# Decoder layer with sorted expert tokens: normalised rows scattered as fp16 halves, sorted tiles turned by the loading DMA, routing tables on GpSimd, two banks for z

## The reference

```python
x = x + attn(layernorm(x), Wqk, bqk, Wv, bv, Wu, bu, Wo, bo, ln_g, ln_b)   # linear attention, 16 heads, gated by silu(u)
x = x + xattn(layernorm(x), tokens, ctx, ctx, ctx)
x = x + ffn(layernorm(x), W_up, W_gate, W_down)
# attn: q = k = elu(x Wqk + bqk); kv = k^T v per head; out = (u * layernorm(q kv; ln_g, ln_b)) Wo + bo
# xattn: expert e = min(token // 6250, 3); W = ctx[e];  y = (silu(n W^T) * (n W^T)) W^T, of the token's own expert
# ffn: ternary weights, q(w) = clip(round(w / mean|w|), -1, 1) * mean|w|; y = (silu(n up^T) * (n gate^T)) down^T
```

## Time and profile before

| | us |
|---|---|
| median of 3 runs (764.87 to 765.67) | 765.36 |
| the profiled execution | 763.66 |
| its span, first to last instruction | 761.9 |
| TensorE busy | 715.7 (94%) |
| VectorE busy | 386.8 (51%) |
| ScalarE busy | 273.1 (36%) |
| GpSimd busy | 131.0 (17%) |
| mean granted TensorE clock | 0.988 of full speed |

### The profile page before, as it was taken

One profiled execution on the slowest core, in us unless ns is written; L12 is line 12 of the kernel. 1 busy time (PEld: TensorE's weight loads), 2 busy tenths in 40 slices (PEclk: granted clock), 3 DMA queues, 4 the chain that ended last, 5 costly groups with the idle time before them and its releaser, 6 DMA issues.

```text
span 761.9 us, 11591 instructions
## 1 busy us (share of the span) xinstructions
PE 715.7 (94%) x3948; PEld 381.1 (50%) x3978; DVE 386.8 (51%) x655; ACT 273.1 (36%) x426; POOL 131.0 (17%) x171
## 2 busy tenths in 40 slices
PE   8998999899899869999998999999999999999993
PEld 6565457457446546666554444444444444444441
DVE  5669766846836746655465333343334333342232
ACT  4365545536436334454322332222222222222220
POOL 4202124404606840000010000020001100020002
PEclk9999999999999999999999999999999999999998
DMA  8924026006207369650102000020001100010001
GB/s 238 343 72 149 1 101 208 23 8 216 108 1 275 126 199 390 240 153 29 29 15 42 15 14 11 4 69 15 14 14 25 58 14 14 15 55 1 0 0 55
DMA packets 48182, 63.99 MB, mean 84 GB/s; under 512 B 25360, under 2 KB 25360, under 8 KB 47120
## 3 DMA queue, kind: packets, MB, share of 16 engines
q1 hardware_dynamic: 43792, 50.89, 21.0%
q0 software_dynamic: 4352, 12.60, 4.3%
HBM read 46.69 MB, written 12.59 MB: 78 GB/s over the span
## 4 chain that ended last, share of the span: by engine, by line
PE 82%; DVE 6%; POOL 4%; issue 3%; ACT 2%; SPq 1%; DMA 1%; DVEq 0%; ACTq 0%; POOLq 0%
PE bank L1342 29%; PE bank L1070 28%; PE bank L1352 14%; PE bank L1063 4%; PE bank L1263 3%; PE bank L1227 2%; DVE late L759 1%; POOL sorted_ids L330 1%; PE bank L1241 1%; POOL sorted_tokens L322 1%; DMA stage<-in_L_attn_Wv_dram 1%; DVE region L606 1%; POOL sorted_residual L326 1%; SPq L190 1%; DVE st L598 1%
## 5 line engine op out<-in xcount | busy, mean ns | idle before, releaser
L1342 PE MATMUL bank<-w_att,region 128*128 128x512 f16 (+1 forms) x1024 | 231.3, 379 | 1.0 <-issue 1.0
L1342 PEld LDWEIGHTS bank<-w_att,region 128*128 (+1 forms) x1024 | 100.1, 98 | 122.0 <-issue 1.5
L1036 DVE SCALAR_TENSOR_TENSOR tmp<-tmp,hk,bank 128x512 f32<-128x512 f32 x64 | 47.8, 747 | 161.6 <-PE bank L1342 161.1
L1352 PE MATMUL bank<-region,tmpA 128*128 (+1 forms) x474 | 116.9, 379 | 1.6
L309 POOL TENSOR_SCALAR ve<-mv 128x1 f32<-128x1 f32 (+1 forms) x37 | 9.5, 256 | 485.0 <-DVE mv L974 336.2
L1070 PE MATMUL bank<-late,w_att 128*128 128x512 f16 x384 | 86.1, 379 | 4.0 <-DVE region L806 3.9
L575 ACT ACTIVATE tmp<-bank,qs 128x512 f32<-128x512 f32 x64 | 44.0, 687 | 122.4 <-PE bank L1342 122.4
L579 ACT ACTIVATE tmpA<-tmp 128x512 f16<-128x512 f32 x64 | 40.3, 629 | 121.5 <-DVE tmp L1036 121.5
L1352 PEld LDWEIGHTS bank<-region,tmpA 128*128 128x128 f16 x504 | 49.2, 98 | 59.6 <-DVE stage L1020 0.9
L1039 DVE TENSOR_TENSOR tmpA<-tmp,tmpA 128x512 f16<-128x512 f32 x64 | 44.4, 693 | 45.6 <-ACT tmpA L579 45.6
L1070 PEld LDWEIGHTS bank<-late,w_att 128*128 128x128 f16 x384 | 37.2, 98 | 46.4 <-DVE region L806 4.7
(11 more groups left out here) (143 smaller groups left out, 813.1 us busy)
## 6 DMA issues: line engine op xcount, KB each, us to landing
stage<-in_L_ffn_W_up_dram SPq DMA_DIRECT2D x8, 1024.0 KB, 5.4
stage<-in_L_ffn_W_gate_dram SPq DMA_DIRECT2D x8, 1024.0 KB, 5.5
stage<-in_ctx_dram SPq DMA_DIRECT2D x4, 1024.0 KB, 6.4
stage<-in_L_ffn_W_down_dram SPq DMA_DIRECT2D x4, 1024.0 KB, 7.3
nrm<-in_L_ffn_W_down_dram SPq DMA_DIRECT2D x4, 1024.0 KB, 7.8
n<-sorted_tokens SPq DMA_DIRECT2D x16, 256.0 KB, 4.2
resid<-sorted_residual SPq DMA_DIRECT2D x4, 1024.0 KB, 9.3
resid<-in_x_dram SPq DMA_DIRECT2D x1, 3072.0 KB, 19.0
```

The source lines that it names most:

```text
L1036: dve.scalar_tensor_tensor(out=h32, in0=sil, scalar=hk[:, 0:1], in1=gate_ps[:, :], op0=ALU.mult, op1=ALU.mult).then_inc(s["hid_mul"], 1)
L1342: mm = pe.matmul(dst, w[:, bass.ds(cf_c, 1), k * P:(k + 1) * P].rearrange("p a n -> p (a n)"), x3T[:, bass.ds(b, 1), i, k].rearrange("p a ...
L1352: mm = pe.matmul(ffy_ps[t][:, :], hid[:, parity, i, t * P:(t + 1) * P], tern[2][:, bass.ds(c, 1)].rearrange("p a n -> p (a n)"), start=(st ...
```

## The change

VectorE no longer makes the step tables; GpSimd does, by 31 dependent instructions and three copies, behind the head roots of batch 0. GpSimd's bias adds wait for the batch's first v_bias. Normalised rows are split into fp16 halves `n2h` (n2_hi on ScalarE, n2_lo on VectorE, laid over region 5) before the scatter, so the sorted rows in DRAM are 2 x 512 fp16 (as many bytes as 512 fp32). The scatter of batch b - 1 moves behind the head roots of batch b, in the last batch behind the last head roots; the scatters of ids all move behind the last residual. ScalarE's first gated half of a batch waits until the scatters before have landed. SP loads each sorted tile by a transposing DMA into x3T, so TensorE's transposes and the splits leave the expert stage; the free bank becomes a second one for z. SP's tile loads wait for z products, and the load of the ids goes last. The last second product stands behind the first up product of the FFN. In the last group of the last batch three down products move behind the last gate and go tile by tile; its last two chunks of hidden halves have a buffer of their own. The filler matmuls of the hand-over go from 70 to 100. The core of the diff:

```diff
+    xs_dram = nc.dram_tensor("sorted_halves", (NT * P, 2 * D), F16, kind="Internal").ap()
...
-    xs_slot = [n2[:, i] for i in range(3)]
+    n2h = region[:, 5].rearrange("p t d -> p (t d)").bitcast(F16).rearrange("p (t h d) -> p t h d", t=T, h=2)
+    sv = w_moe[:, E - 1, 0, 0].bitcast(F32)[:, 0:9 * STEPS].rearrange("p (i j) -> p i j", j=STEPS)
...
+    hid_late = n2[:, 0:2].rearrange("p a d -> p (a d)").bitcast(F16).rearrange("p (i h n) -> p i h n", i=2, h=2)
...
-    z_ps, y_ps, tx_ps, th_ps, q_ps = ps[0], ps[1], ps[2], ps[3], ps[4:8]
+    z_ps, y_ps, th_ps, q_ps = (ps[0], ps[2]), ps[1], ps[3], ps[4:8]
...
         def sorted_tile(i):
-            sp.dma_start(xs_slot[i % 3], xs_v[:, i]).then_inc(s[f"xs_in{i % 3}"], 16)
+            sp.dma_start_transpose(
+                out=x3T[:, i // T, :, :, (i % T) * P:(i % T + 1) * P].rearrange("p i k s -> p (i k) s"),
+                in_=xs_v[i]).then_inc(s[f"xs_in{i % 4}"], 16)
...
-            sp.wait_ge(s["tx_mm"], n + 1)
+            sp.wait_ge(s["z_mm"], n + 1)
...
+        for i in range(9, NT):
+            sp.wait_ge(s["z_mm"], i - 2)
+            sorted_tile(i)
         sp.wait_ge(s["id_sent"], 16 * NT)
         sp.dma_start(row_id[:, :], id_v, allow_slow_non_contiguous=True).then_inc(s["id_in"], 16)
...
-            pool.wait_ge(s["x2_norm"], T * b + t + 1)
-            pool.indirect_dma_start(xs_dram, row_of(T * b + t), n2[:, t], None).then_inc(s["scattered"], 16)
+            pool.wait_ge(s["n2_lo"], T * b + t + 1)
+            pool.indirect_dma_start(xs_dram, row_of(T * b + t), n2h[:, t].rearrange("p h d -> p (h d)"), None).then_inc(s["scattered"], 16)
...
+            pool.wait_ge(s["v_bias"], T * b + 1)
             for t in range(T):
                 pool.tensor_tensor(resid[:, T * b + t], resid[:, T * b + t], bo_bc[:, :], ALU.add).then_inc(s["bias_added"], 1)
             if b > 0:
                 rsqrt(2, "x2_aggr", T * b, slice(0, T), "rs2", b - 1)
             if b < B - 1:
                 rsqrt(0, "x_aggr", T * b + 2 * T, slice(0, T), "rs1", b)
-            if b > 0:
-                for t in range(T):
-                    scatter(b - 1, t)
             if b < B - 1:
                 rsqrt(1, "o_aggr", T * b + T, slice(0, T), "rs_o", b)
             if 0 < b < B - 1:
+                for t in range(T):
+                    scatter(b - 1, t)
+            if b == 0:
+                step_tables()
+            elif b < B - 1:
                 scatter_residual(b - 1)
-                scatter_ids(b - 1)
...
+        def made_by(ins):
+            made[0] += 1
+            ins.then_inc(s["steps_made"], 1)
+            pool.wait_ge(s["steps_made"], made[0])
+        def step_tables():
+            pool.wait_ge(s["route_pos"], 1)
+            pool.wait_ge(s["starts_made"], 3)
+            at, expert, tile, row, of_row, t4 = (sv[:, i] for i in range(6))
+            part = [sv[:, i] for i in range(6, 9)]
...
+            def count_of(dst, src, bounds):
+                for n, bound in enumerate(bounds):
+                    made_by(pool.tensor_scalar(part[n], src, bound, 0.0, ALU.is_ge, ALU.add))
+                made_by(pool.tensor_tensor(dst, part[0], part[1], ALU.add))
+                made_by(pool.tensor_tensor(dst, dst, part[2], ALU.add))
+            count_of(expert, at, [last[:, e:e + 1] for e in range(1, E)])
...
+            count_of(t4, tile, [float(S * m) for m in range(1, B)])
+            made_by(pool.tensor_scalar(t4, t4, float(2 * K * S - S), 0.0, ALU.mult, ALU.add))
+            made_by(pool.tensor_tensor(t4, t4, tile, ALU.add))
+            made_by(pool.tensor_scalar(row, tile, 1.0 / P, 0.0, ALU.mult, ALU.add))
+            pool.tensor_copy(step_off[:, :], t4[0:1]).then_inc(s["route_ready"], 1)
...
+        for t in range(T):
+            scatter(B - 2, t)
         scatter_residual(B - 2)
-        scatter_ids(B - 2)
-        scatter_ids(B - 1)
...
+        for b in range(B):
+            scatter_ids(b)
...
+            if sent is not None:
+                act.wait_ge(s["scattered"], sent)
...
+                if last:
+                    act.wait_ge(s["route_ready"], 3)
...
-                gated_hi(b - 1, 0)
+                gated_hi(b - 1, 0, 16 * T * b - 16 * T)
...
                 magnitudes(b, 1)
+            else:
+                act.wait_ge(s["wo_mm"], T * b)
+                for t in range(T):
+                    n2_hi(b - 1, t)
             o_copies(b)
...
+        def n2_hi(b, t):
+            act.wait_ge(s["x2_norm"], T * b + t + 1)
+            act.activation(n2h[:, t, 0], n2[:, t], ACT.Copy).then_inc(s["n2_hi"], 1)
...
         o_copies(B - 1)
+        for t in range(T):
+            n2_hi(B - 2, t)
         magnitudes(B - 1, 1)
...
-        gated_hi(B - 1, 0)
+        gated_hi(B - 1, 0, 16 * T * (B - 1))
...
+        act.wait_ge(s["wo_mm"], NT)
+        for t in range(T):
+            n2_hi(B - 1, t)
...
-            act.activation(sil, z_ps[:, :], ACT.Silu, scale=1.0 / CTX_SCALE).then_inc(s["z_act"], 1)
-            if i + 1 < NT:
-                xs_hi(i + 1)
...
+                if not (first and cc < 2) and not (ends and cc >= 2):
                     act.wait_ge(s["down_mm"], cf - 1)
-                act.activation(hid[:, cc % 2, 0], h32, ACT.Copy).then_inc(s["hid_hi"], 1)
+                if first and cc == 1:
+                    act.wait_ge(s["y_mm"], STEPS)
+                dst = hid_late if ends and cc >= 2 else hid
+                act.activation(dst[:, cc % 2, 0], h32, ACT.Copy).then_inc(s["hid_hi"], 1)
...
-            route(dve.tensor_copy(pos[:, :], pos_f[:, :]))
-        def routing_steps():
...
+            dve.tensor_copy(pos[:, :], pos_f[:, :]).then_inc(s["route_pos"], 1)
...
+        def n2_lo(b, t):
+            dve.wait_ge(s["n2_hi"], T * b + t + 1)
+            dve.tensor_tensor(n2h[:, t, 1], n2[:, t], n2h[:, t, 0], ALU.subtract).then_inc(s["n2_lo"], 1)
...
-                routing_steps()
+            elif not last:
+                for t in range(T):
+                    n2_lo(b - 1, t)
...
-            if not first:
-                dve.wait_ge(s["scattered"], 16 * T * b)
+            if last:
+                for t in range(T):
+                    n2_lo(b - 1, t)
...
+        dve.wait_ge(s["n2_lo"], T * (B - 1))
         last_sum(0)
         last_sum(1)
         last_norm(0)
         last_sum(2)
         last_norm(1)
+        n2_lo(B - 1, 0)
         last_sum(3)
         last_norm(2)
+        n2_lo(B - 1, 1)
         last_norm(3)
+        n2_lo(B - 1, 2)
+        n2_lo(B - 1, 3)
         dve.wait_ge(s["scatter_out"], 1)
         signs_of(0, 1)
...
-            dve.tensor_tensor(h32, z_ps[:, :], sil, ALU.mult).then_inc(s["h_mul"], 1)
-            if i + 1 < NT:
-                xs_lo(i + 1)
+            dve.tensor_tensor(h32, z_ps[i % 2][:, :], sil, ALU.mult).then_inc(s["h_mul"], 1)
...
-        keep_busy(ps[3], 70)
+        keep_busy(ps[3], 100)
...
-            pe.wait_ge(s["xs_lo"], min(i, NT - 1) + 1)
-            pe.wait_ge(s["h_mul"], i)
-            product(z_ps[:, :], lambda i, j, k: sorted_T[:, bass.ds(off + (i * K + k) * S, P)], w).then_inc(s["z_mm"], 1)
+            if i < NT:
+                pe.wait_ge(s[f"xs_in{i % 4}"], 16 * (i // 4 + 1))
+            if i > 1:
+                pe.wait_ge(s["h_mul"], i - 1)
+            product(z_ps[i % 2][:, :], lambda i, j, k: sorted_T[:, bass.ds(off + (i * K + k) * S, P)], w).then_inc(s["z_mm"], 1)
...
-            if i + 1 < NT:
-                xs_transpose(i + 1)
...
-        second(STEPS - 1)
...
+                if begin:
+                    second(STEPS - 1)
...
-                else:
-                    if begins and cc == 1 and not first:
-                        pe.wait_ge(s["out_made"], T * b)
+                elif not (ends and cc > 0):
+                    if begins and cc == 1:
+                        if first:
+                            pe.wait_ge(s["y_evac"], STEPS)
+                        else:
+                            pe.wait_ge(s["out_made"], T * b)
                     down(cf - 1, c - 1, (cc - 1) % 2, begins and cc == 1, False)
...
+        for t in range(T):
+            for cc in range(4):
+                src = hid if cc < 2 else hid_late
+                for i in range(2):
+                    if t == 0:
+                        pe.wait_ge(s["hid_lo" if i else "hid_hi"], C * B - 3 + cc)
+                    mm = pe.matmul(ffy_ps[t][:, :], src[:, cc % 2, i, t * P:(t + 1) * P], tern[2][:, C - 4 + cc],
+                                   start=False, stop=(cc == 3 and i == 1))
+            mm.then_inc(s["down_last"], 1)
```

More of the change, by code:

```diff
@@ L106, in decoder @@
     tokf = sb("tokf", [P, NT])
-    pad_i = sb("pad_i", [P, 2, E], I32)
-    pad_f = sb("pad_f", [P, 2, E])
+    last = sb("last", [P, E])
     base = sb("base", [P, E])
@@ L161, in decoder @@
         w_hi w_lo ctx_mm ctx_hi ctx_lo abs_done abs_mm scale_step
-        route_step route_mm route_read route_ready
+        route_step route_pos steps_made route_mm route_read route_ready
```

(47 more changed lines are left out.)

74 lines of the change are left out of this document (20 added, 54 removed).

## The result

The changed kernel takes 776.82 us in the median (775.8 to 784.18, 4 runs) against 765.51 for the kernel before in the same comparison: a ratio of 1.0162, 95% interval 1.0096 to 1.0228. I had forecast 759.8, a range of 752.5 to 765.5 and "faster" at 0.81. The result lies outside the range and on the other side. The profiled execution took 775.8 us, span 774.0 (before 763.66 and 761.9, +12.1).

What follows compares the result with a forecast made beforehand. TensorE, carrying 82% of the chain of waits, was taken as the bound. Hand-over +3.2, expert stage -6.0, start of last stage -0.5 and end -2.3 gave -5.6: 758.1 profiled, 759.8 us median, range 752.5 to 765.5.

Steps and rivals of the forecast that it cites:

- Tables: Batch 1: GpSimd makes the tables in 12 us, hidden; third product 2.0 us earlier, head transposes 2.9 us earlier.
- v_bias(1), behind the blocked instruction, comes some 5.6 us late: Attention batches: VectorE blocked by GpSimd's four adds, so the fourth v product waits 2.2 to 2.9 us, taken as 2.6.
- rival A: Attention: adds let VectorE through one at a time, no v product waits, 3 x 2.4 less, 752.6 us; chance 0.20.
- Halves in batches 1 and 2: O products: ScalarE's four n2_hi take 2.5 us, TensorE loses 1.9 us there, 2.1 handed on to the next batch.
- Landings are 2.7 / 4.0 / 6.9 us; ... I take 5.5: Hand-over: batch 2's scatters land in 5.5 us (bounds 2.7 and 9.5), moving gated_hi(3,0) from 247.64 to 251.2, +3.6.
- the first turned tile: Hand-over: the first transposed tile load takes 3.5 us (3.0 to 13.5); first expert product at 282.3, +3.2.
- The ids (16 x 1.27 = 20 us on GpSimd) lie under the experts: Expert stage: the moved id scatters' 20 us of GpSimd issues are hidden under the experts.
- Rival C: Expert stage: turned tiles come too slowly from the queue, z products wait; 771.4 us at 7.0 per tile; chance 0.10.
- Expert stage: Expert steps: each loses a TensorE transpose of 0.44 us, fifteen in the loop; -6.0 us, bounds -5.0 and -6.6.
- end: Last group: down products move behind the last gate, last scatter issued at 751.1 against 753.42; -2.3 us, bounds -1.5 and -2.6.

Runs made afterwards that it cites:

- e8: The kernel of e5 without GpSimd's wait for v_bias(b,0) ahead of the four bias adds of each batch; 773.74 us, ratio 1.011.
- e5: Changed kernel with id scatters held until nine z products are done and the third batch's fp16 halves in a region of their own; 765.61 us, ratio 0.9995.
- e3: Changed kernel with the third batch's fp16 halves in a region of their own, so gated_hi(3,0) waits for no scatter; 770.72 us, ratio 1.0081.
- e12: Changed kernel with only the id scatters moved, to the FFN's first batch; 761.14 us, ratio 0.9952.
- e9: The kernel of e5 with the id scatters moved to the FFN's first batch, eight behind each of two roots; 753.33 us, ratio 0.9835.
- e10: The kernel of e9 plus sixteen spare scatters of 4-byte rows where the change has its ids; 773.2 us, ratio 1.0107.
- e11: The kernel of e9 plus sixteen spare scatters of 512-byte rows where the change has its ids; 753.3 us, ratio 0.9847.
- e4: Changed kernel with sorted tiles loaded by a plain DMA in 256-byte pieces, not transposed; 782.21 us, ratio 1.0228.
- e1: Changed kernel with only the id scatters moved, to behind the ninth z product; 764.48 us, ratio 0.9995.
- e6: Kernel before with all id scatters moved behind the last residual scatter, and SyncE's id load behind the last tiles; 784.5 us, ratio 1.0254.
- e7: Changed kernel with the id scatters back where the kernel before had them; 771.08 us, ratio 1.0081.

## Why the prediction was wrong

**Tables, right.** GpSimd took from 68.28 to 81.4, 13 us where I had 12. The third product of batch 1 stands at 70.79 (70.8), the head transposes at 75.98 (76.1).

**"v_bias(1), behind the blocked instruction, comes some 5.6 us late", wrong, to the good.** I carried the 5.6 us of the earlier trace rows over to another order of instructions. With the adds behind v_bias, VectorE waits for one add at a time, the v products run unbroken, and project(2) comes 7.9 us earlier where I had 1.3. That was rival A, at 0.20. The rule of the Trainium skill ("SBUF — State Buffer", section "Who interferes with whom") that the shared pair is held for one whole instruction agrees with this trace (1.76, 1.16, 1.7); for the 6.30 of e8, two instructions of 0.69 and some 4.9 of waiting, it would need the adds to win four times running. The same section says that the order of issue decides who blocks, and e8 against e5 shows at least that their order decides. Why VectorE loses four times in the one order and once in the other stays open.

**Halves in batches 1 and 2, near.** The new gap in the o products is 1.34 us (I had 1.9), released by ScalarE's copy as said.

**"Landings are 2.7 / 4.0 / 6.9 us; ... I take 5.5", mis-sized, and its start too.** The last scatter landed in 8.7, inside my bound of 9.5. It was issued at 239.33, 6.4 earlier than my sum implies (251.2 - 5.5), since attention came earlier; landing 3.2 later than I took, it let gated_hi(3,0) go at 248.07, 3.1 earlier than the 251.2. The memset stands at 274.15 (I had 276.2). That lead went into the first turned tile, for which I took 3.5 us and which landed in 6.34: the first expert product stands at 282.43, I had 282.3. So three errors nearly cancel, which is luck; a sum that comes out right is no proof of its terms. The scatter wait's own price is 6.1 (e3) to 7.8 (e12).

**"The ids (16 x 1.27 = 20 us on GpSimd) lie under the experts": the step that failed.** I counted the time of the issuing engine, found it free, and costed the move at nothing. I had not asked what the transfers do to other transfers in their new place. They cost 15.7 us (e12), and 17.4 with own halves (e3 against e9); spare ones at the same place cost 19.9 (e10). A sign stood in my own rows: the id scatters, 512 bytes each, took 6.3 to 9.5 us to land, the row scatters of 256 KB only 2.7 to 6.9. Rival C named the right symptom, the turned tiles too slow from the queue, and by its 7.0 us per tile gave 771.4, but its cause was wrong: the turned tiles alone are fast enough. In e12 they land in 5.6 to 11.4 us beside the unit loads and in 3.0 to 4.4 in the late steps, and TensorE waits for none but the first. With the ids away and all else as in the change, the kernel takes 761.1 (e12); my sum was 759.8. That, too, is nearer than its terms were, as the next paragraph shows.

**Expert stage, near by the step, not in the sum; end, right.** Late steps are 5.75 us apart (5.6 to 5.8, one of 6.3). From the fifth tile to the FFN the time fell from 107.85 to 100.95; that includes the steps behind the jam. But without the jam, in e12's profiled execution (762.27), the first to the last z product takes 125.8 us against 127.3 before, 1.5 less where I had 6.0. Its first product runs at half clock, as above (5.30 for 2.76, 2.5 us that my sum lacks), and one late step takes 7.6 us, 1.8 more than its neighbours; why is not shown. From the first gate to the end it is 2.2 us less (I had 2.3). Two slips of arithmetic weigh little: 10 x 0.44 + 5 x 0.3 is 5.9 and not 6.0, and rival C's tile of 6.3 us gives 766.5, 1.1 above the kernel before and not over 1.5.

## What to carry to other kernels

Moving a DMA moves its traffic as well as its issue. Ask of each moved transfer how small its rows are and what else is in flight in the new place, the loads of the next stage and the engines' instructions among it; here the scatters of 4-byte rows cost nothing where the engines run in loops and little is loaded (e9), and scatters of 512-byte rows cost nothing even beside the loads (e11). When a change has several parts, an error that helps can pay for one that harms, so check terms one by one: here -6.4 (scatters issued earlier), +3.2 (their landing), +2.8 (the first tile) and +15.7 (the ids) hid in one number. And before a buffer is reused behind a scatter, look whether another is free: 6 to 8 us came from a change of layout alone.

## What was unexpected of the hardware

- Sixteen scatters of 128 rows of 4 bytes each, issued over 20 us, cost 15.7 to 19.9 us beside 1 MB loads; the same with rows of 512 bytes, which also lie further apart, cost nothing (773.2 against 753.3; e9 753.3). In two windows of 4 us the DMA rate is 54 and 85 GB/s in the change, 0 and 40 in e4, and 373 and 398 in e1, where the ids are not beside the loads. The Trainium skill, page "DMA: Bandwidth & Descriptors", section "Why small descriptors are slow (HBM only)", gives every packet a fixed overhead of about 3 cycles and every DMA operation 32 bytes of metadata. An estimate from that page's figure: if each of the 2048 rows is one operation, they add 64 KB of metadata, little beside a single load of 1 MB. The measurement says otherwise and decides. What in the path of a 4-byte write is so slow is not shown here.
- While they run, engines can stand still that wait for no data (TensorE 1 us per instruction by "issue" in e6 and e5, ScalarE 5.81 and VectorE 4.35 by "remote" in e7), but need not (the changed kernel, e1). The page of the profile lists two instruction queues among the DMA queues, so I take it that the fetching of instructions is held up too. It fits that nothing of the kind appears in the FFN's loops (e9), but there little is loaded either, so that is no proof; no run here took the fetches away.
- The four bias adds of GpSimd block a VectorE instruction either for one add or for all four, by the order in which they meet: 8.1 us of the kernel's time hang on one wait (e8).
